# Routed rows of a mixture-of-experts layer: scattered into slot order, or gathered by block from token order

## The chip, the cores and the metric

One core of a Trainium2 chip, one launch. The metric is the device time of that core in microseconds (us). The kernel runs cross-attention and a mixture-of-experts feed-forward layer on 2048 tokens of width 512, four batches of 512.

## The reference, cut to what matters

```python
x = x + xattn(_layernorm(x), ctx_1024, ...)        # 16 heads, not touched by the change
xt = _layernorm(x).reshape(-1, 512)                # N = 2048 tokens
gate = xt @ Wr + br                                # 7 routed experts
_, ids = jax.lax.top_k(gate + gate_bias, 2)        # two experts for each token
probs = softmax(gate at ids, -inf elsewhere)
for e in range(7):                                 # e-th routed expert
    u = xt @ Wup[e] + bup[e]
    g = silu(u @ Wgate[e] + bgate[e]) * u
    eo[e] = g @ Wdown[e] + bdown[e]
out = sum_e probs[:, e] * eo[e] + shared_expert(xt)   # one shared expert of the same form
x = x + out
```

The kernel computes an expert only for the tokens that chose it: 4096 rows, grouped by expert and padded to blocks of 128, at most 38 blocks.

## The kernel before, in words

Five stages follow one another with a barrier of all engines after each: `project` (projections of the attention), `attend` (scores, softmax, values), `output` (output projection, second layer norm, routing, and the shared expert for the first eight tiles of tokens), `routed` (38 blocks of routed expert work) and `late` (the shared expert for the other eight tiles, and the sum of everything). There is no planner: each engine has its own instruction list, written out by hand, and semaphores join them.

In `output`, TensorE multiplies tile by tile (16 tiles of 128 tokens; `attended`, `turn`, `scores`). VectorE (DVE) writes the normed rows of a tile into `xn2` (L1311). Then TensorE does the shared expert in two groups of four tiles: `up` (8 products), `prefix` (two small products that count tokens by expert), `gate(0, c)`, `gate(1, c)` and `down(0, j)`, `down(1, j)`, c and j from 0 to 3, each of 12 matmuls of 128x512 (L1515). A `down(0, j)` waits for all four `gated_low(0, c)` of DVE (L1357). DVE has, in this order: the logits and the two maxima, a long chain of small operations that ends in `slot` (L1429, the place of each token's two rows in the array sorted by expert), `up_low(1, 3)`, `gated` and `gated_low` of group 0, the tables of blocks (L1438 to L1445), the same of group 1, and `down`. ScalarE (ACT) alternates `gate` and `gated_hi`. GpSimd (POOL) waits for `slot` and issues 32 indirect DMAs (L1241), each of which scatters a tile's 128 rows of `xn2` into `xs_dram`, and waits until they have landed. `xs_dram` has 38 x 128 rows; the rows of padding slots have to be zero, so in `attend` SyncE (SP) writes 38 blocks of zeros to it (L816) from a zero tile.

In `routed`, SP loads block n of `xs_dram` (256 KB, L1628) into one of two buffers. TensorE's step n (L1773) is: `up` product of block n (12 matmuls), half of `down` of block n - 2, transposes of block n - 1's `g` and of block n's `u`, the other half of `down`, then the four transposes of the rows of block n + 1 (`psX`, L1753; they wait for the load), and the `gate` product of block n. ACT's L1690 copies each transposed block out of PSUM. POOL meanwhile loads the experts' weights and splits each into two half-precision parts: 42 halves of a matrix (experts 2 to 7 and the shared one again, seven times six), for each the pieces L193, L197, L198, L201 and then the load of the half after next (L183) in the same queue. Four experts' worth (24 halves) are in a hardware loop with one operation more (L1674); the last 18 are written out. A block's first product waits for the split of its expert. The last copy of the shared expert waits for 16 blocks (L1684). SP stores a block's result to `ys_dram`; `late` gathers from there with 32 indirect DMAs (L1887) of the same kind as the new ones.

Of the kernel before, what the change touches and what calls it, by code (L numbers as in the profile page):

```python
# [21 lines left out]
F32 = mybir.dt.float32  # L22
F16 = mybir.dt.float16
# [35 lines left out]
UNROLL = 4  # L59
E_EARLY = 2  # L60
# [26 lines left out]
def build(nc, t, out, upto=99, dbg=None):  # L87
# [17 lines left out]
    with ctx:  # L105
# [5 lines left out]
        xs_dram = dram("xs_dram", (NSLOT, D), F32)  # L111
# [13 lines left out]
        CONST = 2848 + 256 + 2 * HD * 4 + 2 * 32  # L125
# [11 lines left out]
        blk_w = const("blk_w", [P, NBLK], I32)  # L137
        ws_tile = const("ws_tile", [P, 1], F32)
# [7 lines left out]
        wo = nc.alloc_sbuf_tensor_at("wo", [P, 2, KD, D], F16, offset=WO_AT)  # L146
        V_AT = (WO_AT - V_BYTES) // 32 * 32
# [3 lines left out]
        zero = nc.alloc_sbuf_tensor_at("zero", [P, D], F32, offset=O_AT + (B - 1) * KD * 2 * S * 2)  # L151
# [22 lines left out]
        xs_zeroed = sem("xs_zeroed")  # L174
# [570 lines left out]
def attend(nc, t, sem, g_):  # L745

    ident_b, ones, v_all, oT_all, q_stk, k_stk, q_hi, k_hi, zero, loaded, hi_loaded = (
        g_[k] for k in "ident_b ones v_all oT_all q_stk k_stk q_hi k_hi zero stk_loaded hi_loaded".split())
# [21 lines left out]
    zeroed = sem("a_zeroed")  # L770
    CLEAR_AT = 2 * G

    with ExitStack() as ps:  # L773
# [18 lines left out]
        @block.sync  # L792
        def _(sp):
            pair = TB // PAIR - 1
            for buf, dst, done, parts in ((g_["q_st"], q_dram, g_["qk_stored"][0], (0, 0, 1)), (g_["k_st"], k_dram, g_["qk_stored"][1], (0, 1, 0))):
                for r, part in enumerate(parts):
                    d = dst[r, (B - 1) * D:B * D, pair * PAIR * P:(pair + 1) * PAIR * P]
                    sp.dma_start(d.rearrange("(c p) t -> p c t", p=P), buf[:, pair, part]).then_inc(done[pair], 16)
            for u in range(N):
                if u == 2 * G - 1:  # L800
                    for q in g_["qk_stored"][0] + g_["qk_stored"][1]:
                        sp.wait_ge(q, 3 * 16 * NT // PAIR // 2)
                n = u - CLEAR_AT
                if n == 0:
                    sp.wait_ge(zeroed, 1)
# [12 lines left out]
            sp.wait_ge(g_["split_done"], len(early) + 1)  # L818
            sp.dma_start(raw[:, 0, :], t["x"].rearrange("b s d -> (b s) d")[0:P, :]).then_inc(g_["x0_loaded"], 16)
            sp.dma_start(raw[:, 1, :], t["L0_xattn_bo"].partition_broadcast(P)).then_inc(g_["bo_loaded"], 16)  # L820

        @block.gpsimd
        def _(pool):

            pool.memset(nm[:, :, :, :], 0.0).then_inc(s["nm0"], 1)
            pool.memset(zero[:, :], 0.0).then_inc(zeroed, 1)
            pool.wait_ge(zeroed, 1)
# [46 lines left out]
        def _(act):  # L874
# [17 lines left out]
            def hi_part(gr):  # L892
                b, c = divmod(gr, KD)
                act.wait_ge(s["o_sum"], gr + 1)
                if b == B - 1 and c == 0:
                    act.wait_ge(g_["xs_zeroed"], 16 * NBLK)
# [183 lines left out]
def output(nc, t, sem, g_):  # L1080

    w_exp, ident, oT_all, wo, slot, prob, pmat, blk_k, blk_w, b_up, b_gate = (
        g_[k] for k in "w_exp ident oT_all wo slot prob pmat blk_k blk_w b_up b_gate".split())
# [55 lines left out]
    sqrt_first = sb("sqrt_first", [P, 1], F32)  # L1139
    names = """r_loaded bo_copied br_loaded col_loaded xb_r y_mm x1_r stats aggr veps sd_r rs_r xn_r nT_t nT_c r_mm logit  # L1140
        xT_h xT_l u_mm u_r u_h u_l g_mm silu g_r g_h g_l d_mm d_r
        const0 const1 iota member prefix exp_in exp slots probs scattered"""
# [15 lines left out]
    with ExitStack() as ps:  # L1158
# [16 lines left out]
        def _(sp):  # L1175
# [42 lines left out]
        def _(pool):  # L1218
# [6 lines left out]
            pool.iota(bidx_i[:, :], pattern=[[1, NBLK]], base=0, channel_multiplier=0).then_inc(s["iota"], 1)  # L1225
            pool.wait_ge(s["const0"], 1)
# [71 lines left out]
        def _(dve):  # L1298
# [35 lines left out]
            for n in range(NT + 2):  # L1334
                if n == TB:
                    dve.wait_ge(s["iota"], 2)
                    link(dve.tensor_copy(ramp[:, :], ramp_i[:, :]))
                    link(dve.tensor_copy(bidx[:, :], bidx_i[:, :]))
                    dve.wait_ge(s["bo_copied"], 1)
# [131 lines left out]
        def _(pe):  # L1471
# [102 lines left out]
def routed(nc, t, sem, g_):  # L1574

    w_exp, blk_k, blk_w, ident, seen, ws_tile, bias = (
        g_[k] for k in "w_exp blk_k blk_w ident seen ws_tile bias".split())
    tag = "e_"
    N = NBLK
    sb = Map(nc, SBUF_LO + E * g_["PER_E"], g_["AUX_AT"])  # L1580
    x_in = sb(tag + "x", [P, 2, D], F32)
# [9 lines left out]
    x_ld = [sem(tag + "x_loaded0"), sem(tag + "x_loaded1")]  # L1591
# [23 lines left out]
    with ExitStack() as ps:  # L1615
# [6 lines left out]
        def _(sp):  # L1622
# [36 lines left out]
        def _(pool):  # L1659
# [436 lines left out]
```

## Time and profile before

| | us |
|---|---|
| three runs | 1059.81, 1060.17 (median), 1060.41 |
| the profiled execution: its time | 1063.63 |
| its span, from first to last instruction | 1062.0 |
| mean granted TensorE clock | 0.96 of full |

A row of instructions gives the line, the engine, the operation and the tiles it writes and reads, and then counts and times. A name with a q (POOLq, SPq) is the engine's own sequencer: barriers, branches, the issue of DMAs. A DMA's time to landing is from its issue until its semaphore has risen. All times in rows are us from the start of the span, unless marked ns.

### The profile page before, as it was taken

How to read it: one execution, taken by the hardware profiler on the slowest of the kernel's cores; microseconds unless marked ns; L12 is line 12 of the kernel's file. 1: busy time of each engine (PE TensorE's matmuls, PEld its weight loads, DVE VectorE, ACT ScalarE, POOL GpSimd, SP SyncE). 2: the span in 40 equal slices, each digit the busy share in tenths (PEclk: the TensorE clock that was granted, in tenths of full speed). 3: DMA queues.
4: the chain of work that ended last, by engine and by line, in shares of the span. 5: the costliest groups of instructions: out<-in, count | busy, mean ns of one | idle time of the engine just before them, and what ended most of it. 6: DMA issues, size and time to landing. Idle time of an engine off the chain costs nothing. (4 is left out here: it accounts for less than half of the span.)

```text
span 1062.0 us, 17127 instructions
## 1 busy us (share of the span) xinstructions
PE 925.9 (87%) x5077; PEld 404.0 (38%) x5078; DVE 653.6 (62%) x1022; ACT 464.8 (44%) x844; POOL 614.1 (58%) x554
## 2 busy tenths in 40 slices
PE   1789894698988988879999389999999999999898
PEld 1345452111111211136644134454455444554343
DVE  5877774777877878447766145455545545443288
ACT  2365663667767777622353012322232223232440
POOL 0465556257667676443107488899899999000660
PEclk9899997599999999989999689999999999999899
DMA  7134445234444431123325754565556655444763
GB/s 262 35 103 132 137 135 168 70 134 175 146 170 166 142 110 62 51 72 134 132 83 219 278 159 159 186 198 176 177 180 198 187 175 171 119 119 179 279 198 139
DMA packets 104521, 162.31 MB, mean 153 GB/s; under 512 B 10904, under 2 KB 53912, under 8 KB 104080
## 3 DMA queue, kind: packets, MB, share of 16 engines
q1 hardware_dynamic: 90240, 115.13, 34.1%
q0 software_dynamic: 12896, 45.10, 12.2%
q10 hardware_dynamic: 1328, 1.36, 0.4%
q8 instruction: 30, 0.49, 0.2%
q14 instruction: 27, 0.22, 0.1%
HBM read 108.08 MB, written 53.48 MB: 152 GB/s over the span
## 5 line engine op out<-in xcount | busy, mean ns | idle before, releaser
L933 DVE TENSOR_REDUCE nm<-a_psS 128x4 bf16<-128x1984 f32 x64 | 142.7, 2229 | 63.8 <-PE a_psS L992 61.9
L890 ACT ACTIVATE p_t<-a_psT 128x512 f32<-128x512 f32 x256 | 138.9, 595 | 64.8 <-PE a_psT L1009 63.1
L843 POOL TENSOR_TENSOR p_sum<-p_t,p_t 128x512 f32<-128x512 f32 x64 | 81.4, 1273 | 93.6 <-ACT p_t L890 92.7
L1763 PE MATMUL e_psU<-w_exp,e_xT 128*128 x456 | 107.4, 386 | 7.6 <-issue 3.4
L1763 PE MATMUL e_psY<-w_exp,e_gT 128*128 x456 | 110.7, 379 | 0.9 <-ACT e_y L1704 0.9
L1763 PE MATMUL e_psG<-w_exp,e_uT 128*128 x456 | 106.5, 384 | 2.5 <-DVE e_uT L1718 2.5
L201 POOL TENSOR_TENSOR w_exp<-e_raw,w_exp 128x1024 f32 (+1 forms) x42 | 90.1, 2144 | 6.0 <-POOL e_raw L198 4.5
L1009 PE MATMUL a_psT<-q_stk,k_stk 98*128 98x512 f16 x256 | 85.8, 400 | 4.0 <-ACT p_t L890 1.5
L193 POOL TENSOR_TENSOR w_exp<-e_raw,ws_tile 128x1024 f32 (+1 forms) x42 | 80.2, 1909 | 6.1 <-DMA e_raw<-in_L_ffn_Wup_dram 5.2
L1690 ACT ACTIVATE e_gT<-e_psGT 128x512 f16<-128x512 f32 x38 | 22.7, 597 | 125.1 <-PE e_psGT L1753 125.1
L1745 DVE TENSOR_TENSOR e_g<-e_g,e_u 128x512 f32<-128x512 f32 x38 | 58.8, 1547 | 26.4 <-ACT e_g L1711 26.4
L1711 ACT ACTIVATE e_g<-e_g 128x512 f32<-128x512 f32 x38 | 23.9, 630 | 107.8 <-DVE e_g L1721 107.8
L1763 PEld LDWEIGHTS e_psU<-w_exp,e_xT 128*128 128x128 f16 x456 | 42.1, 99 | 71.8 <-issue 27.9
L1016 PE MATMUL a_psO<-p_t,v_all 128*32 128x512 f32 x512 | 68.8, 611 | 0.1
L1763 PEld LDWEIGHTS e_psG<-w_exp,e_uT 128*128 128x128 f16 x456 | 42.3, 99 | 54.5 <-issue 10.4
L1763 PEld LDWEIGHTS e_psY<-w_exp,e_gT 128*128 128x128 f16 x456 | 44.5, 98 | 46.6 <-issue 1.4
L1009 PEld LDWEIGHTS a_psT<-q_stk,k_stk 98*128 98x128 f16 x256 | 17.9, 97 | 111.4 <-issue 67.3
L1241 POOL DMA_INDIRECT xs_dram<-xn,slot x32 | 31.4, 980 | 48.5 <-DVE slot L1429 39.1
L1721 DVE SCALAR_TENSOR_TENSOR e_g<-e_psG,bias 128x512 f32<-128x512 f32 x38 | 26.3, 692 | 53.7 <-PE e_psG L1763 53.7
L1718 DVE TENSOR_TENSOR e_xT<-e_psX,e_xT 128x512 f16<-128x512 f32 x38 | 26.3, 691 | 50.0 <-ACT e_xT L1690 50.0
L1718 DVE TENSOR_TENSOR e_gT<-e_psGT,e_gT 128x512 f16<-128x512 f32 x38 | 26.3, 692 | 47.8 <-ACT e_gT L1690 47.8
L1485 PE MATMUL o_psY<-wo,oT_all 128*128 128x512 f16 x192 | 45.3, 388 | 6.0 <-PEq L773 6.0
(317 smaller groups left out, 1792.8 us busy)
## 6 DMA issues: line engine op xcount, KB each, us to landing
xs_dram<-zero SPq DMA_DIRECT2D x38, 256.0 KB, 5.3
e_x<-xs_dram SPq DMA_DIRECT2D x38, 256.0 KB, 4.1
bias<-in_L_ffn_bup_dram SPq DMA_DIRECT2D x38, 256.0 KB, 3.7
bias<-in_L_ffn_bgate_dram SPq DMA_DIRECT2D x38, 256.0 KB, 3.9
ys_dram<-e_y SPq DMA_DIRECT2D x38, 256.0 KB, 4.0
q_dram<-q_st SPq DMA_DIRECT2D x24, 256.0 KB, 2.9
k_dram<-k_st SPq DMA_DIRECT2D x24, 256.0 KB, 3.7
q_stk<-q_dram SPq DMA_DIRECT2D x64, 96.0 KB
```

Source lines behind the costliest of these rows:

```text
L193: pool.tensor_tensor(hi, w, ws, ALU.mult).then_inc(w_scaled, 1)
L201: pool.tensor_tensor(lo, w, hi, ALU.subtract).then_inc(split_done, 1)
L843: pool.tensor_tensor(p_sum[:, w % SUMS, :], probs(w, 0), probs(w, 1), ALU.add).then_inc(s["sum_1"], 1)
L890: act.activation(probs(w, k), psT[:, k % 2], ACT.Exp, scale=SCALE / (QS * QS)).then_inc(s["exp"], 1)
L933: dve.tensor_reduce(nm[:, i, :, 0:1].rearrange("p h o -> p (h o)"), psS[:, :, 0:NMAIN], AX.X, ALU.max, negate=True)
L1009: pe.matmul(psT[:, k % 2], k_stk[0:KR, w % SLOTS, k * P:(k + 1) * P], q_stk[0:KR, w % SLOTS, :], start=True, stop=True).then_inc(s["t_mm"], 1)
L1016: ins = pe.matmul(dst[j * HD:(j + 1) * HD, :], stationary(n), moving(n), start=first, stop=last, tile_position=(0, j * HD))
L1241: pool.indirect_dma_start(g_["xs_dram"], bass.IndirectOffsetOnAxis(ap=slot[:, k, n:n + 1], axis=0), xn2[:, n, :], None).then_inc(s["scatte ...
L1485: ins = pe.matmul(psY[n % 2][:, :], oT_all[:, b, q, x, j * P:(j + 1) * P], wo[:, y, q, :], start=(i == 0), stop=(i == len(terms) - 1))
L1718: return dve.tensor_tensor(pair[:, 1], src[:, :].rearrange("p (k n) -> p k n", n=P), pair[:, 0], ALU.subtract)
L1745: dve.tensor_tensor(g[:, :], g[:, :], u[:, j], ALU.mult).then_inc(s["g_r"], 1)
L1763: ins = pe.matmul(dst[:, :], stationary, moving, start=(k == 0 and chunks[0] == 0), stop=(k == len(terms) - 1 and chunks[-1] == KD - 1))
```

## The change

`xs_dram`, its 38 clears, the zero tile and the 32 scatters are taken out. In their place the normed rows go to `xn_dram` in token order, tile by tile, by SP. DVE and TensorE make a table `token`: for each block (38 columns) and each row of it (128 partitions) the number of the token. It comes from one-hot matrices: with `at_row` (row of the slot, 128 columns) as stationary and `at_blk` (block of the slot times the token's number, 38 columns) as moving operand, 32 small matmuls add up the table in PSUM, after `gate(1, 2)`; DVE copies it to SBUF after `gated_low(0, 0)`. Padding slots get token 0; nothing reads their results. POOL gathers the rows of block n with an indirect DMA into `x_rows[n % 2]`: blocks 0 and 1 at the end of its `output` list, the other 36 between the halves of its weight splitting in `routed`. There POOL's loop is now written out for all 42 halves, without L1674's operation. The rows' buffers are where `wo` was.

```diff
+ROWS = 2
-        xs_dram = dram("xs_dram", (NSLOT, D), F32)
+        xn_dram = dram("xn_dram", (B * S, D), F32)
+        def gather(pool, n):
+            pool.indirect_dma_start(x_rows[:, n % ROWS, :], None, xn_dram,
+                                    bass.IndirectOffsetOnAxis(ap=token[:, n:n + 1], axis=0)).then_inc(row_ld[n % ROWS], 16)
 # attend: SP
-                if 0 <= n < NBLK:
-                    sp.dma_start(g_["xs_dram"][n * P:(n + 1) * P, :], zero[:, :]).then_inc(g_["xs_zeroed"], 16)
 # output: SP, after the store of x1 and the load of a tile
+                if n:
+                    sp.wait_ge(s["xn_r"], n)
+                    sp.dma_start(g_["xn_dram"][(n - 1) * P:n * P, :], xn2[:, n - 1, :]).then_inc(s["xn_stored"], 16)
 # output: POOL (and two iotas more at its start)
-            pool.wait_ge(g_["xs_zeroed"], 16 * NBLK)
-            pool.wait_ge(s["xn_r"], NT)
-            pool.wait_ge(s["slots"], 1)
-            for k in range(TOP):
-                for n in range(NT):
-                    pool.indirect_dma_start(g_["xs_dram"], bass.IndirectOffsetOnAxis(ap=slot[:, k, n:n + 1], axis=0),
-                                            xn2[:, n, :], None).then_inc(s["scattered"], 16)
-            pool.wait_ge(s["scattered"], 16 * TOP * NT)
+            pool.wait_ge(s["xn_stored"], 16 * NT)
+            pool.wait_ge(s["tokens"], 1)
+            for n in range(ROWS):
+                g_["gather"](pool, n)
 # output: DVE
-            dve.tensor_copy(slot[:, :, :], slot_f[:, :, :]).then_inc(s["slots"], 1)
+            link(dve.tensor_copy(slot[:, :, :], slot_f[:, :, :]))
             up_low(1, 3)
+            link(dve.tensor_scalar(in_blk_i[:, :, :], slot[:, :, :], 7, None, ALU.logical_shift_right))
+            link(dve.tensor_copy(in_blk[:, :, :], in_blk_i[:, :, :]))
+            link(dve.scalar_tensor_tensor(in_row[:, :, :], in_blk[:, :, :], -float(P), slot_f[:, :, :], ALU.mult, ALU.add))
+            for k in range(TOP):
+                dve.tensor_tensor(at_row[:, k], ... [P, NT, P], ... [P, NT, P], ALU.is_equal)
+                link(dve.tensor_tensor(at_blk[:, k], ... [P, NT, NBLK], ... [P, NT, NBLK], ALU.is_equal))
+                dve.tensor_tensor(at_blk[:, k], at_blk[:, k], tok ... [P, NT, NBLK], ALU.mult).then_inc(s["places"], 1)
             for c in range(KD):
                 gated(0, c)
                 if c:
                     gated_low(0, c - 1)
+                if c == 1:
+                    dve.wait_ge(s["places_mm"], 1)
+                    dve.tensor_copy(token[:, :], psR[:, 0:NBLK]).then_inc(s["tokens"], 1)
 # output: TensorE
+            def tokens():
+                pe.wait_ge(s["places"], TOP)
+                for k in range(TOP):
+                    for n in range(NT):
+                        ins = pe.matmul(psR[:, 0:NBLK], at_row[:, k, n, :], at_blk[:, k, n, :], ...)
+                ins.then_inc(s["places_mm"], 1)
             for c in range(KD):
                 gate(1, c)
+                if c == 2:
+                    tokens()
 # routed: SP loses load(n, j), three lines; POOL:
                         for piece in range(3):
                             g_["split_half"](...)
+                        for b in range(ROWS, N):
+                            if (b - ROWS) * 4 // 3 == (k - E_EARLY) * 2 * NM + 2 * m + half:
+                                pool.wait_ge(s["xT_t"], b - ROWS + 1)
+                                g_["gather"](pool, b)
...
-                        if not isinstance(k, int):
-                            pool.tensor_tensor(seen[:, :], ws_tile[:, :], ws_tile[:, :], ALU.add)
                         load(*((k, half, m + 1) if m < NM - 1 else (k + 1, half, 0)))
-            with pool.Fori(E_EARLY, E - 1) as k:
+            for k in range(E_EARLY, E + 1):
                 halves(k, False)
-            halves(E - 1, False)
-            halves(E, False)
             pool.wait_ge(s["y_mm"], B * S // P)
             halves(E + 1, True)
+            for b in range(ROWS, N):
+                if (b - ROWS) * 4 // 3 >= 2 * NM * (E + 2 - E_EARLY):
+                    pool.wait_ge(s["xT_t"], b - ROWS + 1)
+                    g_["gather"](pool, b)
```

## Rows read from the trace of the kernel before

**Rows 1.** The busy time of each engine by stretch; the columns stand in its first line.

```profile
core 0: us, PE busy (x) PEld busy (x) DVE busy (x) ACT busy (x) POOL busy (x), PEclk, DMA share, GB/s
592.00:607.00 15.00, 0.12 (x1) 0.12 (x2) 0.69 (x1) 0.00 (x0) 7.26 (x8) 0.58 0.56 204
607.00:985.00 378.00, 362.87 (x1824) 181.38 (x1824) 185.32 (x228) 107.42 (x190) 265.76 (x232) 0.99 0.54 171
...
607.00:612.00 5.00, 3.37 (x10) 1.48 (x11) 0.69 (x1) 0.60 (x1) 0.64 (x1) 0.50 0.90 315
```

**Rows 2.** The same view inside `attend`: beside the clears, and after them.

```profile
274.00:300.00 26.00, 22.15 (x156) 4.74 (x157) 19.26 (x23) 18.62 (x34) 18.20 (x15) 1.00 0.49 169
...
404.00:430.00 26.00, 21.87 (x157) 4.72 (x156) 19.33 (x19) 17.86 (x33) 14.59 (x12) 1.00 0.19 61
```

**Rows 3.** The end of `output` by engine (min/median/max ns, first and last start).

```profile
L1158 SPq DRAIN  x1: 7/7/7, 596.4 to 596.4; - x1
L1158 POOLq COMPARE_BRANCH  x1: 46/46/46, 601.0 to 601.0; - x1
L1158 POOLq DRAIN  x1: 2667/2667/2667, 601.2 to 601.2; - x1
```

**Rows 4.** Timeline around that end: start us, us, instructions, idle before and its releaser.

```profile
586.42 5.34 PE L1515 MATMUL o_psN<-w_exp,f_gT 128*128 128x512 f16 x24
...
592.74 0.69 DVE L1364 SCALAR_TENSOR_TENSOR o_y<-o_psN,o_x_again 128x512 f32<-128x512 f32 x1 [2.09 <-DMA x_dram<-o_y]
...
604.59 1.55 POOL L183 DMA_DIRECT2D e_raw<-in_L_ffn_Wup_dram  x2 [5.35 <-POOLq L1158]
...
606.88 1.12 PE L1753 MATMUL e_psX<-ident,e_x 128*128 128x128 f32 x4 [15.12 <-DMA e_x<-xs_dram]
...
611.36 1.88 POOL L193 TENSOR_TENSOR w_exp<-e_raw,ws_tile 128x1024 f32 x1 [5.22 <-DMA e_raw<-in_L_ffn_Wup_dram]
```

**Rows 5.** Timeline of the middle of `output`, where the table's operations go in.

```profile
558.02 1.29 DVE L1353 TENSOR_TENSOR f_g<-f_g,f_u 128x512 f32<-128x512 f32 x2
...
560.52 5.34 PE L1515 MATMUL o_psE<-f_uT,w_exp 128*128 128x512 f16 x24
...
563.43 0.39 DVE L1438 TENSOR_TENSOR cmpb<-bidx,cum_a 128x228 f32<-128x228 f32 x1
...
570.88 5.34 PE L1515 MATMUL o_psN<-w_exp,f_gT 128*128 128x512 f16 x24
```

**Rows 6.** Groups by line: busy us, mean ns of one, idle us before.

```profile
L648 DVE SCALAR_TENSOR_TENSOR wq<-wq_raw,wq 128x2048 f16<-128x2048 f32 x1 | 2.3, 2293 | 2.0 <-ACT wq L518 2.0
L999 PE MATMUL a_psX<-ident_b,nm 128*128 128x128 bf16 x64 | 6.6, 228 | 3.8 <-DVE nm L934 2.5
L1887 POOL DMA_INDIRECT l_yr<-ys_dram,slot x32 | 34.2, 1067 | 9.9 <-issue 9.9
L1241 POOL DMA_INDIRECT xs_dram<-xn,slot x32 | 31.4, 980 | 48.5 <-DVE slot L1429 39.1 <-issue 9.4
```

**Rows 7.** The landing of the 32 indirect DMAs of `late`.

```profile
DMA to landing us min/median/max: 3.4/4.1/7.9
```

**Rows 8.** L193 alone in a stretch of 15 written-out halves, first start to sixteenth.

```profile
791.92:892.89 100.97, 28.66 (x15) 1.00 0.58 183
```

**Rows 9.** Timeline of one written-out half on POOL.

```profile
811.27 0.77 POOL L183 DMA_DIRECT2D e_raw<-in_L_ffn_Wdown_dram  x1 [0.30 <-POOL w_exp L201]
812.07 1.90 POOL L193 TENSOR_TENSOR w_exp<-e_raw,ws_tile 128x1024 f16<-128x1024 f32 x1
...
815.44 2.13 POOL L201 TENSOR_TENSOR w_exp<-e_raw,w_exp 128x1024 f16<-128x1024 f32 x1
817.87 0.77 POOL L183 DMA_DIRECT2D e_raw<-in_L_ffn_Wup_dram  x1 [0.30 <-POOL w_exp L201]
```

**Rows 10.** ACT's copies of blocks 2 to 32, and TensorE's transposes of block 32.

```profile
L1690 ACT ACTIVATE e_xT<-e_psX x31: 591/591/592, 626.9 to 917.2; 128x512 f16<-128x512 f32 x31
...
916.51 0.60 PE L1753 MATMUL e_psX<-ident,e_x 128*128 128x128 f32 x4
```

More of the change, by code:

```diff
@@ L124, in build @@
         O_BYTES = B * KD * 2 * S * 2
-        CONST = 2848 + 256 + 2 * HD * 4 + 2 * 32
+        CONST = 2848 + 256 + 2 * HD * 4 + 2 * 32 + 160
         const = Map(nc, SBUF_HI - CONST, SBUF_HI)
@@ L137, in build @@
         blk_w = const("blk_w", [P, NBLK], I32)
+        token = const("token", [P, NBLK], I32)
         ws_tile = const("ws_tile", [P, 1], F32)
@@ L146, in build @@
         wo = nc.alloc_sbuf_tensor_at("wo", [P, 2, KD, D], F16, offset=WO_AT)
+        x_rows = nc.alloc_sbuf_tensor_at("x_rows", [P, ROWS, D], F32, offset=WO_AT)
         V_AT = (WO_AT - V_BYTES) // 32 * 32
@@ L150, in build @@
         oT_all = nc.alloc_sbuf_tensor_at("oT_all", [P, B, KD, 2, S], F16, offset=O_AT)
-        zero = nc.alloc_sbuf_tensor_at("zero", [P, D], F32, offset=O_AT + (B - 1) * KD * 2 * S * 2)
         half_sb = Map(nc, SBUF_LO, V_AT)
@@ L173, in build @@
         hi_loaded = [sem(f"hi_loaded{n}") for n in range(2)]
-        xs_zeroed = sem("xs_zeroed")
+        row_ld = [sem(f"rows_loaded{n}") for n in range(ROWS)]
         split_done = sem("w_split_done")
@@ L745, in attend @@
 def attend(nc, t, sem, g_):
-    ident_b, ones, v_all, oT_all, q_stk, k_stk, q_hi, k_hi, zero, loaded, hi_loaded = (
-        g_[k] for k in "ident_b ones v_all oT_all q_stk k_stk q_hi k_hi zero stk_loaded hi_loaded".split())
+    ident_b, ones, v_all, oT_all, q_stk, k_stk, q_hi, k_hi, loaded, hi_loaded = (
+        g_[k] for k in "ident_b ones v_all oT_all q_stk k_stk q_hi k_hi stk_loaded hi_loaded".split())
     q_dram, k_dram = g_["q_dram"], g_["k_dram"]
@@ L769, in attend @@
     raw_ld = sem("a_raw_loaded")
-    zeroed = sem("a_zeroed")
-    CLEAR_AT = 2 * G
     with ExitStack() as ps:
@@ L825, in _ @@
             pool.memset(nm[:, :, :, :], 0.0).then_inc(s["nm0"], 1)
-            pool.memset(zero[:, :], 0.0).then_inc(zeroed, 1)
-            pool.wait_ge(zeroed, 1)
+            pool.wait_ge(s["nm0"], 1)
             pool.memset(k_stk[K3:KR, :, :], QS).then_inc(s["sel"], 1)
@@ L894, in hi_part @@
                 act.wait_ge(s["o_sum"], gr + 1)
-                if b == B - 1 and c == 0:
-                    act.wait_ge(g_["xs_zeroed"], 16 * NBLK)
                 if b == B - 1 and c == 1:
@@ L1080, in output @@
 def output(nc, t, sem, g_):
-    w_exp, ident, oT_all, wo, slot, prob, pmat, blk_k, blk_w, b_up, b_gate = (
-        g_[k] for k in "w_exp ident oT_all wo slot prob pmat blk_k blk_w b_up b_gate".split())
+    w_exp, ident, oT_all, wo, slot, prob, pmat, blk_k, blk_w, b_up, b_gate, token = (
+        g_[k] for k in "w_exp ident oT_all wo slot prob pmat blk_k blk_w b_up b_gate token".split())
     low = Map(nc, SBUF_LO + E_EARLY * g_["PER_E"], g_["O_AT"])
@@ L1139, in output @@
     sqrt_first = sb("sqrt_first", [P, 1], F32)
+    row_i = sb("row_i", [P, P], I32)
+    row = sb("row_f", [P, P], F32)
+    tok_i = sb("tok_i", [P, NT], I32)
+    tok = sb("tok_f", [P, NT], F32)
+    in_blk_i = sb("in_blk_i", [P, TOP, NT], I32)
+    in_blk = sb("in_blk", [P, TOP, NT], F32)
+    in_row = sb("in_row", [P, TOP, NT], F32)
+    at_row = sb("at_row", [P, TOP, NT, P], F16)
+    at_blk = sb("at_blk", [P, TOP, NT, NBLK], F16)
     names = """r_loaded bo_copied br_loaded col_loaded xb_r y_mm x1_r stats aggr veps sd_r rs_r xn_r nT_t nT_c r_mm logit
         xT_h xT_l u_mm u_r u_h u_l g_mm silu g_r g_h g_l d_mm d_r
-        const0 const1 iota member prefix exp_in exp slots probs scattered"""
+        const0 const1 iota member prefix exp_in exp slots probs xn_stored places places_mm tokens"""
     s = {n: sem("o_" + n) for n in names.split()}
@@ L1225, in _ @@
             pool.iota(bidx_i[:, :], pattern=[[1, NBLK]], base=0, channel_multiplier=0).then_inc(s["iota"], 1)
+            pool.iota(row_i[:, :], pattern=[[1, P]], base=0, channel_multiplier=0).then_inc(s["iota"], 1)
+            pool.iota(tok_i[:, :], pattern=[[P, NT]], base=0, channel_multiplier=1).then_inc(s["iota"], 1)
             pool.wait_ge(s["const0"], 1)
@@ L1335, in _ @@
                 if n == TB:
-                    dve.wait_ge(s["iota"], 2)
+                    dve.wait_ge(s["iota"], 4)
                     link(dve.tensor_copy(ramp[:, :], ramp_i[:, :]))
                     link(dve.tensor_copy(bidx[:, :], bidx_i[:, :]))
+                    link(dve.tensor_copy(row[:, :], row_i[:, :]))
+                    link(dve.tensor_copy(tok[:, :], tok_i[:, :]))
                     dve.wait_ge(s["bo_copied"], 1)
@@ L1428, in _ @@
                 link(dve.tensor_reduce(slot_f[:, k, :], prod[:, :, :], AX.X, ALU.add))
-            dve.tensor_copy(slot[:, :, :], slot_f[:, :, :]).then_inc(s["slots"], 1)
+            link(dve.tensor_copy(slot[:, :, :], slot_f[:, :, :]))
             up_low(1, 3)
+            link(dve.tensor_scalar(in_blk_i[:, :, :], slot[:, :, :], 7, None, ALU.logical_shift_right))
+            link(dve.tensor_copy(in_blk[:, :, :], in_blk_i[:, :, :]))
+            link(dve.scalar_tensor_tensor(in_row[:, :, :], in_blk[:, :, :], -float(P), slot_f[:, :, :], ALU.mult, ALU.add))
+            for k in range(TOP):
+                dve.tensor_tensor(at_row[:, k], row[:, :].unsqueeze(1).broadcast_to([P, NT, P]),
+                                  in_row[:, k, :].unsqueeze(2).broadcast_to([P, NT, P]), ALU.is_equal)
+                link(dve.tensor_tensor(at_blk[:, k], bidx[:, :].unsqueeze(1).broadcast_to([P, NT, NBLK]),
+                                       in_blk[:, k, :].unsqueeze(2).broadcast_to([P, NT, NBLK]), ALU.is_equal))
+                dve.tensor_tensor(at_blk[:, k], at_blk[:, k], tok[:, :].unsqueeze(2).broadcast_to([P, NT, NBLK]), ALU.mult).then_inc(s["places"], 1)
             for c in range(KD):
@@ L1560, in _ @@
             up(0, 3)
+            def tokens():
+                pe.wait_ge(s["places"], TOP)
+                for k in range(TOP):
+                    for n in range(NT):
+                        ins = pe.matmul(psR[:, 0:NBLK], at_row[:, k, n, :], at_blk[:, k, n, :],
+                                        start=(k == 0 and n == 0), stop=(k == TOP - 1 and n == NT - 1))
+                ins.then_inc(s["places_mm"], 1)
             for c in range(KD):
@@ L1574, in routed @@
 def routed(nc, t, sem, g_):
-    w_exp, blk_k, blk_w, ident, seen, ws_tile, bias = (
-        g_[k] for k in "w_exp blk_k blk_w ident seen ws_tile bias".split())
+    w_exp, blk_k, blk_w, ident, seen, ws_tile, bias, x_in, x_ld = (
+        g_[k] for k in "w_exp blk_k blk_w ident seen ws_tile bias x_rows row_ld".split())
     tag = "e_"
     N = NBLK
-    sb = Map(nc, SBUF_LO + E * g_["PER_E"], g_["AUX_AT"])
-    x_in = sb(tag + "x", [P, 2, D], F32)
+    sb = Map(nc, SBUF_LO + E * g_["PER_E"], g_["WO_AT"])
     xT = sb(tag + "xT", [P, 2, 2, KD, P], F16)
@@ L1590, in routed @@
     s = {n: sem(tag + n) for n in names.split()}
-    x_ld = [sem(tag + "x_loaded0"), sem(tag + "x_loaded1")]
     raw_ld = [sem("e_raw_loaded0"), sem("e_raw_loaded1")]
@@ L1624, in rows @@
                 return g_[name][ds(n * P, P), :]
-            def load(n, j):
-                at_least(sp, s["xT_t"], n - 1)
-                sp.dma_start(x_in[:, j], rows("xs_dram", n)).then_inc(x_ld[j], 16)
             def biases(n):
@@ L1637, in step @@
             def step(n, j, i):
-                if not isinstance(n, int) or n + 2 < N:
-                    load(n + 2, j)
                 if live(n, -1):
@@ L1649, in step @@
                     sp.dma_start(g_["of_first"][:, :, :], g_["x1_dram"][0:NBASE * P, :].rearrange("(n p) d -> p n d", p=P)).then_inc(late_ld, 16)
-            load(0, 0)
             biases(0)
-            load(1, 1)
             run(sp, step)
```

3 lines of the change are left out of this document (removed).

## The prediction, made before the changed kernel was run

> **What bounds the kernel now.** I read the busy times by stretch first. In `routed`, 378 of the 1062 us of span, TensorE is busy 362.87 us at a granted clock of 0.99: its own work bounds the stage. POOL is busy 265.76 us there and has slack only because it stops early (of its 42 halves the last but one begins at 892.89) [rows 1, 8]. The one large hole is ahead of it: from 592 to 607 TensorE does 0.12 us of work [rows 1]. The view of the stage's end shows who is late: TensorE ends at 591.8, DVE at 593.4, SP reaches the barrier at 596.4, but POOL sees its scatters landed only at 601.0 and then drains for 2.67 us [rows 3, 4]. Then SP issues the load of block 0 and TensorE starts at 606.88 [rows 4]. So the scatters cost TensorE about 8 us past SP's end, plus nearly 3 us for a load that could have been made before. After the hole the granted clock is 0.50, the lower of its two levels, 1.2 of 2.4 GHz, from 607 to 612 [rows 1].
>
> **The clears.** 38 writes and SP's issues vanish from `attend`. Beside them TensorE is busy 22.15 of 26 us, after them 21.87, at one clock [rows 2]: they were hidden by TensorE's and DVE's work, and nothing comes back. I take 0; both signs of 1 us are possible.
>
> **The rows' stores and the constants.** 16 DMA issues of SP and two iotas fall beside tile work that TensorE bounds; SP waits there for DVE, not the reverse. Taken as 0, at most 1 us.
>
> **The table on DVE.** Ahead of `gated(0, 0)` come two operations of 128x2048 at 2.29 us [rows 6], four of 128x608 and three small ones. The 608 columns lie between 228 at 0.39 and 512 at 0.69 [rows 5] and above: 0.8 each. With 0.2 for each small one that is 4.6 + 3.2 + 0.6 = 8.4 us. Less than 4 would need half the price of each row, more than 10 a disturbed DVE. So `gated(0, 0)` moves from 558.0 to 566.4 [rows 5].
>
> **The table on TensorE.** 32 matmuls with a weight load each. The nearest row is L999's, 0.228 us for one of 128 columns; such matmuls overlap, and four transposes take 0.60 together with the end of the last [rows 6, 10], so some 0.11 each. I take 0.107, 3.4 us in all; the ends are 3.2 and 32 x 0.228 = 7.3. TensorE comes to them after `gate(1, 2)` at 560.5 + 7.8 = 568.3, when DVE is done at 566.4, ends at 571.7, and `gate(1, 3)` at 574.3. DVE stands at its wait with `gated(0, 2)`, `gated(0, 3)` and all of group 1 behind it. It goes on at 571.9 and needs two pairs of 1.4 us and the last `gated_low`: 575.4. `down(0, 0)` waits for that, so it starts at 575.4 instead of 570.88 [rows 5]: 4.5 us later. Group 1's `gated` (6.5 us from 578.3) is ready just before `down(1, 0)` at 585.8. TensorE ends at 591.8 + 4.5 = 596.3.
>
> **The boundary.** The last `down` of DVE ends near 597.0. DVE had waited 2.1 us for stores that shared the DMAs with the scatters [rows 4]; that cover is gone, and a store should land in some 2.3 us. SP ends at 599.3. POOL has nothing outstanding, so no long drain. Its load came 0.7 us after its drain's end before [rows 3, 4]: 600.1 now, against 604.59, 4.5 us earlier. TensorE has its rows already and starts at 599.9, 7.0 us earlier. With a shorter hole the lower clock should cost about 1.5 us less (it now takes some 5). By TensorE alone the sum would be -8.5 us.
>
> **The gathers, and what is late next.** POOL had 42 halves; now 36 gathers stand between them or behind. The loop's extra operation goes, so all halves cost what the written-out ones do: 100.97 / 15 = 6.73 us [rows 8]. Of one gather, `late` shows 1.067 us busy and 9.9 / 32 = 0.31 idle before it, pitch 1.36 beside a busy DVE; the scatters show 0.98 + 0.30 [rows 6, 7]. Behind L201 the load waits 0.30 for its completion [rows 9], and a gather in between could cover that. So a gather adds 0.98 at least and 1.45 at most; I take 1.3, near the pitch, as I see nothing that makes the sequencer's pause overlap.
>
> The gather of block b stands behind half (b - 2) x 4 // 3: the gaps are one, one and two halves. Three blocks therefore cost POOL 4 x 6.73 + 3 x 1.3 = 30.8 us. TensorE needs (917.2 - 626.9) / 30 = 9.68 us a block, 29.0 for three [rows 10]. POOL is the slower by 1.8 us every three blocks, and TensorE comes to wait, at its `psX` transposes, for blocks 5, 8, 11 and so on; all it does afterwards is behind that wait, the `gate` product first. Block 32's gather (b - 2 = 30) stands behind half 40, the last one that comes after a pair. POOL's first split follows its load by 6.77 us [rows 4], at 606.9. The gather of block 2 follows that split by 5.8, at 612.7. That of block 32 follows by 40 x 6.73 + 30 x 1.3 = 308.2: 920.9. It lands 3.8 us later (3.4 to 4.1 in rows 7): 924.7. Before, these transposes began at 916.51 [rows 10]. So TensorE is 8.2 us later there, not 8.5 earlier. Block 33's gather is one half later and no wait; the last four follow without a half between them. The remainder and `late` keep their length. The weights' splits slow down too: six halves and four or five gathers are 46 us an expert, against 2 x 2048 / 7 = 585 rows, five padded blocks and 48 us of TensorE. The second expert is split at 606.9 + 46 = 653, and the first one's five or six blocks end near 650 to 658: at most a wait of a few us, which the rows' later waits would swallow. The rows bind.
>
> The Trainium skill, in "DMA: Bandwidth & Descriptors", section "Anatomy of one DMA — SWDGE (gpsimd) path", speaks against this: it calls descriptor generation "small, variable" and says that many descriptors can be emitted before it shows. By that rule a gather would cost POOL next to nothing and the sum would be rival 1's. Of this the trace says otherwise: POOL is held for about a microsecond by each indirect DMA [rows 6], so I stay with the rows.
>
> Sum, against the profiled execution: span 1062.0 + 8.2 = 1070.2, and with its 1.6 us around the span 1071.8 in place of 1063.63. The median of the runs is 3.5 us below the profiled time; the same step from 1060.17 gives 1068.4 us.
>
> **Rivals.** (1) POOL keeps up and the gain stays. For it: slack in POOL of 80 us at the end, and a loop's overhead removed. It needs 4h + 3g below 29.0 us and an early lead, as with g = 0.98 and h = 6.55. Then TensorE bounds as before: -8.5, 1051.7. With g = 0.98 and h = 6.73 the price falls by 30 x 0.32 = 9.6: -1.4, a result of no size. (2) POOL is dearer still: a gather at 1.45 and the weight load behind it in the same queue landing late, since a half's load has 7.4 us [rows 9] and the gather's 256 KB go first. The price is 30 x 0.15 = 4.5 and 40 x 0.1 = 4: 1077. It decides from the first block on which TensorE waits, near block 5. [...] (3) The table doesn't shorten the boundary: the stage's end stays near 604, since SP's last store or a drain after the two gathers takes the place of the scatters. Against it: the gathers are issued near 572. It would add 3 to 4 us to the forecast, within its range.
>
> **How the numbers follow.** The forecast's own range, +3 to +12 (1063 to 1072), has 0.53; rival 1 with its lesser gains, -9 to -2, 0.27; rival 2 0.14; 0.06 is left for sums near zero. A change of under 0.2% (2 us) can't be told from none. Faster: 0.28, same 0.05, slower 0.67. The range takes in most of rivals 1 and 2: 1052 to 1077.
>
> **What would show it.** Right: the hole ahead of `routed` some 4 us of TensorE instead of 15; TensorE waiting about 2 us for `x_rows` at every third block and at no other; POOL busy without idle time to some 930; the last `down` of `output` near 596. Wrong: TensorE's pitch at 9.7 with no waits on `x_rows`, or halves with a gather not over 1.1 us longer than those without. If TensorE waits at the `up` product for L201 instead, the splits bind and not the rows.

## The result

| | before | changed |
|---|---|---|
| median of the runs, us | 1059.66 (1057.32 to 1061.35, 20 runs) | 1061.61 (1060.85 to 1064.79, 20 runs) |
| the profiled execution: time, span | 1063.63, 1062.0 | 1063.08, 1061.3 |

The ratio is 1.0023, 95% interval 1.0015 to 1.0031: 2 us slower. The forecast was 8.2 us slower, 1068.4. The direction held by a hair, and a later repeat can't tell it from no change (1.0007, below). The size did not hold: 6.8 us too high. The measured time lies inside the stated range of 1052 to 1077, which is wide enough for most outcomes.

First the busy times of the changed kernel by stretch, in the columns of [rows 1]:

```profile
592.00:607.00 15.00, 7.97 (x29) 3.30 (x28) 3.46 (x5) 0.60 (x1) 2.67 (x3) 0.77 0.63 190
607.00:985.00 378.00, 355.58 (x1813) 178.89 (x1811) 182.53 (x227) 107.10 (x188) 298.84 (x244) 1.00 0.52 167
607.00:612.00 5.00, 3.16 (x18) 1.66 (x17) 1.98 (x3) 1.09 (x2) 4.59 (x5) 1.00 0.39 144
```

The hole has shrunk: TensorE has 7.97 us of work in those 15, where it had 0.12. It then has 7.3 us less work in `routed` in the same 378 us, and POOL 33 us more. The granted clock from 607 to 612 is full, not half.

Next, the middle of `output` in the changed kernel, as a timeline (it answers to [rows 5]). L1444 to L1448 are the table on DVE, L1586 is the table on TensorE, L1456 its copy, and the last row is `down(0, 0)`.

```profile
560.64 2.29 DVE L1444 TENSOR_TENSOR at_row<-row_f,in_row 128x2048 f16<-128x2048 f32 x1
...
562.85 0.78 DVE L1446 TENSOR_TENSOR at_blk<-bidx,in_blk 128x608 f16<-128x608 f32 x1
...
568.11 1.28 DVE L1362 TENSOR_TENSOR f_g<-f_g,f_u 128x512 f32<-128x512 f32 x2
...
570.13 0.97 PE L1586 MATMUL o_psR<-at_blk,at_row 128*128 128x38 f16 x32
...
571.14 0.20 DVE L1456 CAST token<-o_psR 128x38 int32<-128x38 f32 x1 [0.96 <-PE o_psR L1586]
...
574.67 1.67 PE L1536 MATMUL o_psN<-w_exp,f_gT 128*128 128x512 f16 x7 [0.98 <-DVE f_gT L1366]
```

Then the barrier of `output` by engine (it answers to [rows 3]), and the timeline around it (to [rows 4]):

```profile
L1164 POOLq DRAIN  x1: 5051/5051/5051, 572.4 to 572.4; - x1
...
L1164 SPq DRAIN  x1: 7/7/7, 600.7 to 600.7; - x1
```

```profile
597.70 0.69 DVE L1373 SCALAR_TENSOR_TENSOR o_y<-o_psN,o_x_again 128x512 f32<-128x512 f32 x1 [1.40 <-DMA x_dram<-o_y]
...
600.95 1.09 PE L1776 MATMUL e_psX<-ident,x_rows 128*128 128x128 f32 x4 [5.40 <-PEq L1164]
601.37 1.51 POOL L185 DMA_DIRECT2D e_raw<-in_L_ffn_Wup_dram  x2 [26.60 <-POOLq L1164]
...
605.85 1.89 POOL L195 TENSOR_TENSOR w_exp<-e_raw,ws_tile 128x1024 f16<-128x1024 f32 x1 [2.96 <-DMA e_raw<-in_L_ffn_Wup_dram]
...
611.50 1.06 POOL L217 DMA_INDIRECT x_rows<-xn_dram,token  x1 [0.17 <-issue]
```

SP, not POOL, now ends the stage; POOL's drain of 5 us lies at 572, hidden. TensorE starts at 600.95 instead of 606.88.

Inside `routed`, POOL's timeline (it answers to [rows 9]): a half with a gather, and below the dots the start of one without. After it the window of L195 alone, 16 halves with 12 gathers (to [rows 8]).

```profile
790.56 2.13 POOL L203 TENSOR_TENSOR w_exp<-e_raw,w_exp 128x1024 f16<-128x1024 f32 x1
792.85 1.32 POOL L217 DMA_INDIRECT x_rows<-xn_dram,token  x1 [0.17 <-issue]
794.17 0.76 POOL L185 DMA_DIRECT2D e_raw<-in_L_ffn_Wgate_dram  x1
794.96 1.91 POOL L195 TENSOR_TENSOR w_exp<-e_raw,ws_tile 128x1024 f16<-128x1024 f32 x1
...
816.49 0.77 POOL L185 DMA_DIRECT2D e_raw<-in_L_ffn_Wdown_dram  x1 [0.30 <-POOL w_exp L203]
```

```profile
787.18:907.64 120.46, 30.49 (x16) 1.00 0.54 174
```

And who waits: TensorE's waits in `routed` (us in total, times, longest), and after it, from the timeline, the gather of block 32 and its transposes (to [rows 10]).

```profile
PE e_psX L1776 <- DMA x_rows<-xn_dram,token: 7.2, 7, 1.8
PEld e_psX L1776 <- DMA x_rows<-xn_dram,token: 11.9, 10, 2.3
PE e_psGT L1776 <- DVE e_g L1768: 5.1, 7, 1.1
```

```profile
913.32 1.32 POOL L217 DMA_INDIRECT x_rows<-xn_dram,token  x1 [0.17 <-issue]
...
917.34 0.66 PE L1776 MATMUL e_psX<-ident,x_rows 128*128 128x128 f32 x4 [0.69 <-DMA x_rows<-xn_dram,token]
```

PEld is TensorE's weight load, which comes just ahead of the matmul. It waits for the rows at ten blocks: 5, 8, 11 and so on to 32, every third and no other. From its first split (605.85) to the gather of block 32 POOL itself never waits longer than 0.3 us. Block 32's transposes start at 917.34, where they started at 916.51: TensorE began `routed` 5.9 us earlier and is 0.8 us later here. So POOL's list of halves and gathers is the bound, and a gain of some 6 to 8 us was given back in it.

In these two profiled executions what follows is 1.5 us shorter than before, so the spans differ by -0.7; the medians differ by +2.0. The size has to come from the medians: a second trace of the kernel before (the repeat below) has block 32's transposes at 913.54 and a span of 1056.0, where the first has 916.51 and 1062.0. A second trace of the changed kernel starts `output` 2.9 us later (469.3 against 466.3), and its span is 1064.0.

### The profile page after: what moved, and what is told of

Read it like the earlier page. It is cut to its first block and busy times, and to the rows that moved or that the text cites. A ratio compares the mean times of both kernels' runs of the same rounds, so it can differ in the third digit from the quotient of the medians.

```text
span 1061.3 us, 16869 instructions
## 1 busy us (share of the span) xinstructions
PE 924.7 (87%) x5109; PEld 404.3 (38%) x5110; DVE 659.5 (62%) x1034; ACT 464.9 (44%) x844; POOL 617.9 (58%) x537
## 3 DMA queue, kind: packets, MB, share of 16 engines
q10 hardware_dynamic: 1328, 1.36, 0.4%
## 5 line engine op out<-in xcount | busy, mean ns | idle before, releaser
L203 POOL TENSOR_TENSOR w_exp<-e_raw,w_exp 128x1024 f16<-128x1024 f32 x42 | 90.0, 2143 | 3.5
L217 POOL DMA_INDIRECT x_rows<-xn_dram,token x38 | 43.0, 1131 | 78.8 <-DVE token L1456 50.5
L195 POOL TENSOR_TENSOR w_exp<-e_raw,ws_tile 128x1024 f16<-128x1024 f32 x42 | 80.0, 1906 | 4.0 <-DMA e_raw<-in_L_ffn_Wup_dram 3.0
L1768 DVE TENSOR_TENSOR e_g<-e_g,e_u 128x512 f32<-128x512 f32 x38 | 56.5, 1488 | 26.4 <-ACT e_g L1734 26.4
```

The source lines that it names most:

```text
L195: pool.tensor_tensor(hi, w, ws, ALU.mult).then_inc(w_scaled, 1)
L203: pool.tensor_tensor(lo, w, hi, ALU.subtract).then_inc(split_done, 1)
L1768: dve.tensor_tensor(g[:, :], g[:, :], u[:, j], ALU.mult).then_inc(s["g_r"], 1)
```

## The experiments

Theory A, after the result: POOL binds in `routed` as forecast, but a gather costs it less than the 1.3 us taken. Theory B: POOL doesn't bind, and the loss comes from elsewhere (shared DMAs, the written-out loop, the removed clears).

**One gather per 1.25 halves, or per 1.5.** Only the places of the gathers move; POOL has the same work in total.

```diff
-                            if (b - ROWS) * 4 // 3 == (k - E_EARLY) * 2 * NM + 2 * m + half:
+                            if (b - ROWS) * 5 // 4 == (k - E_EARLY) * 2 * NM + 2 * m + half:
```

(The same in the condition of the last gathers. The other kernel has `3 // 2` at both places.)

> The changed kernel with each gather one place earlier on average: block b's gather stands behind half (b - 2) x 5 // 4 instead of x 4 // 3; the work is the same. Theory (GpSimd's pace holds TensorE in the routed stage): four blocks then cost GpSimd 5 x 6.73 + 4 x 1.07 = 37.9 us against TensorE's 38.7, so TensorE never waits for rows; block 32's transposes come about 9.5 us earlier than in the kernel before and the time is 8 to 10 us below the changed kernel, near 1052. Rival (the gain is lost to slower gathers or other contention of the DMAs, not to the order on GpSimd): within 2 us of the changed kernel, as the same transfers are made. Rival (the weights' splits bind once they are later): waits of the up product for L203, a gain of under 5 us.

> The changed kernel with the gathers rarer: behind half (b - 2) x 3 // 2. Theory: two blocks cost GpSimd 3 x 6.73 + 2 x 1.07 = 22.3 us against 19.4 of TensorE, so TensorE waits some 2.9 us at every second block from block 4 or 6 on, and is 28 us later at block 32 than in the kernel before: 27 to 29 us over the changed kernel, near 1089. Rival (the DMAs, not the order): no change within 2 us.

Measured: with 5 // 4 1051.82 us, ratio 0.9936 (0.9923 to 0.995); with 3 // 2 1089.5 us, ratio 1.0283 (1.0269 to 1.0298). The waits of TensorE in `routed` of the kernel with 3 // 2:

```profile
PE e_psX L1776 <- DMA x_rows<-xn_dram,token: 26.9, 13, 3.4
```

With 5 // 4 this list has no row for `x_rows`. One constant moves the time by 10 us down or 28 up from the changed kernel, both as expected, so where the gathers stand in POOL's list decides: theory A. Not all of the 10 us are waits for rows: from the changed kernel to 5 // 4 these fall from 7.2 us to none, and TensorE's waits for DVE's product (`e_psGT`) from 5.1 to 0.9. Why the product is faster there is taken up in the last section.

**The rows loaded by SP instead of gathered.** In place of all gathers SP loads 128 consecutive rows of `xn_dram` (the wrong tokens, so the routed part is computed from other rows); the table is still made.

```diff
-                                g_["gather"](pool, b)
+                        sp.dma_start(x_in[:, j], g_["xn_dram"][ds((n + 2) * 48, P), :]).then_inc(x_ld[j], 16)
```

> The changed kernel with no gather at all: SyncE loads each block's 128 rows in one piece from the stored rows, at the place where the kernel before loaded them (the rows are not those of the block's tokens, so the outputs differ). The table is still made. Theory: GpSimd has only its halves (6.73 us each), TensorE bounds the routed stage, and the time is that of e1, 1050 to 1053. Rival (the loss is in the output stage or at its end): within 2 us of the changed kernel.

Measured: 1052.68 us, ratio 0.994 (0.9926 to 0.9954). Its POOL timeline, load and first piece of two neighbouring halves:

```profile
787.50 0.78 POOL L185 DMA_DIRECT2D e_raw<-in_L_ffn_Wdown_dram  x1 [0.30 <-POOL w_exp L203]
788.31 1.91 POOL L195 TENSOR_TENSOR w_exp<-e_raw,ws_tile 128x1024 f16<-128x1024 f32 x1
...
794.12 0.78 POOL L185 DMA_DIRECT2D e_raw<-in_L_ffn_Wdown_dram  x1 [0.30 <-POOL w_exp L203]
794.92 1.91 POOL L195 TENSOR_TENSOR w_exp<-e_raw,ws_tile 128x1024 f16<-128x1024 f32 x1
```

Here a half takes 6.74 us in the mean over the written-out loop (6.61 in these rows); in the changed kernel 120.46 / 16 = 7.53 with three gathers to four halves. So a gather costs POOL (7.53 - 6.74) / 0.75 = 1.06 us. Behind a gather the load has no wait of 0.30, and the gather's own pause is 0.17. And with the gathers gone TensorE keeps its gain: this kernel and the one with 5 // 4 lie within 1 us of each other (within 2 us of its repeat below).

**Before, with POOL's loop written out.** The hardware loop goes, and its extra operation with it, and nothing else.

```diff
-            with pool.Fori(E_EARLY, E - 1) as k:
+            for k in range(E_EARLY, E + 1):
```

> The kernel before with GpSimd's loop over four experts written out, as the change has it, and nothing else. Theory: GpSimd isn't what TensorE waits for there, so the halves get shorter (7.2 to 6.7 us) and the time stays within 1.5 us of the kernel before. Rival (the written-out loop itself costs, through its code): over 2 us slower.

Measured: 1061.16 us, ratio 1.0014 (1.0005 to 1.0023). The halves that were in the loop fell from 7.23 to 6.73 us, as forecast for the changed kernel, but before that wasn't the bound: a faster POOL alone brings nothing. The time rose by 1.8 us, 0.3 more than expected, and I can't place that. The changed kernel has the same written-out loop, so part of its own +2.0 may come from there; no run separates the two.

**Four kernels on another chip.** The next four ran on a chip on which the kernel before takes 1100.91 us (1098.36 to 1103.94, 11 runs), so they are compared with each other: from the changed kernel with the clears put back (last of the four) to the others.

Plain loads on POOL in place of the 36 gathers of `routed` (consecutive rows, so again the wrong tokens):

```diff
-                                g_["gather"](pool, b)
+                                pool.dma_start(x_in[:, b % ROWS], g_["xn_dram"][b * 48:b * 48 + P, :]).then_inc(x_ld[b % ROWS], 16)
```

> The changed kernel with the 36 gathers of the routed stage replaced by plain loads of 128 stored rows in one piece, issued by GpSimd at the same places (the rows are not those of the block's tokens, so the outputs differ). Theory: only the gather's price on GpSimd differs, some 0.78 us instead of 1.07; three blocks cost it 4 x 6.73 + 3 x 0.78 = 29.3 us against TensorE's 29.0, so TensorE hardly waits and the time is 7 to 9 us below the changed kernel, 1053 to 1055. Rival (the wait is for the landing of the rows, any transfer on this queue behind the splits): under 2 us below the changed kernel.

One small operation on POOL behind each gather:

```diff
                                 g_["gather"](pool, b)
+                                pool.tensor_tensor(seen[:, :], ws_tile[:, :], ws_tile[:, :], ALU.add)
```

> The changed kernel with one small GpSimd operation more behind each gather of the routed stage (128x1, like L199: 0.19 us and a gap of some 0.08), which brings a gather's share from the measured 1.07 to 1.34 us, near the 1.3 that was forecast. Theory (the forecast's only wrong term was this price): block 32 comes 30 x 0.27 = 8 us later and the time is 7 to 9 us over the changed kernel, 1069 to 1071. Rival (TensorE's waits absorb it, or other terms were wrong by as much): under 4 us over.

The table later, behind `gated` of group 0 on DVE and in `down(0, 1)` on TensorE, with 5 // 4:

```diff
-                if c == 2:
-                    tokens()
...
+                if j == 1:
+                    tokens()
```

> Experiment e1 (gathers behind half (b - 2) x 5 // 4) with the table made later: DVE's operations for it come after group 0's gated_low, its matmuls after down(0, 1), and DVE copies the table after group 1's gated_low. Theory: down(0, 0) no longer waits for the table (about 2 us from e1, 1.0 of it matmuls that stay), so the output stage ends 1 to 2 us earlier and the time is 1 to 2 us below e1, near 1050.5. Rival (group 1's gated_low becomes what down(1, 0) waits for): the same as e1 or up to 2 us slower.

The clears and their zero tile put back into `attend`:

```diff
+                if 0 <= n < NBLK:
+                    sp.dma_start(g_["xs_dram"][n * P:(n + 1) * P, :], zero[:, :]).then_inc(g_["xs_zeroed"], 16)
```

> The changed kernel with the 38 clears of an unused array put back into the attention stage, with their zero tile, issues and the wait of ScalarE for them. Theory: they are hidden, so the time is that of the changed kernel within 1 us. Rival (the removal of 10 MB of writes had given something back, or had moved the stage's end, which is 1.3 us later in the changed kernel's trace): over 1.5 us from the changed kernel.

Measured: 1079.01, 1092.98, 1080.75 and 1087.68 us; ratios to before 0.9793 (0.9769 to 0.9817), 0.9928 (0.9912 to 0.9945), 0.9806 (0.9777 to 0.9835), 0.9885 (0.9863 to 0.9906). Plain loads are 8.7 us below the kernel with the clears, as expected. The small operation is 5.3 above it, not 7 to 9, but not under 4 either. POOL's timeline of these two kernels, the plain load first, shows why:

```profile
787.61 0.61 POOL L1693 DMA_DIRECT2D x_rows<-xn_dram  x1
788.22 0.71 POOL L185 DMA_DIRECT2D e_raw<-in_L_ffn_Wgate_dram  x1
788.95 1.91 POOL L195 TENSOR_TENSOR w_exp<-e_raw,ws_tile 128x1024 f16<-128x1024 f32 x1
```

```profile
792.78 1.07 POOL L217 DMA_INDIRECT x_rows<-xn_dram,token  x1 [0.17 <-issue]
793.86 0.21 POOL L1694 TENSOR_TENSOR seen<-ws_tile 128x1 f32<-128x1 f32 x1
793.99 0.76 POOL L185 DMA_DIRECT2D e_raw<-in_L_ffn_Wgate_dram  x1
```

The added operation is 0.21 us long, but the load behind it starts 0.13 after it, not 0.21 or more: it overlaps too. Over 30 gathers 0.13 makes 3.9 us. Counted from the first split, block 32's copy comes 4.4 us later than in the kernel with the clears, and 3.2 later than in the changed kernel on the first chip. This is POOL's bound tested by a dose: what is added per gather comes back some 30 times at block 32. The whole time is the weaker measure here, since on this chip the two traces also differ by 4 us after block 32.

The clears: in the stretch of `attend` beside them (274 to 300, columns as in [rows 1]), first the kernel that has them back, then the changed one:

```profile
274.00:300.00 26.00, 22.12 (x160) 4.72 (x156) 19.33 (x21) 18.57 (x35) 18.99 (x16) 1.00 0.49 169
```

```profile
274.00:300.00 26.00, 22.17 (x160) 4.74 (x160) 19.26 (x23) 18.60 (x35) 17.76 (x15) 1.00 0.32 107
```

The DMA share falls from 0.49 to 0.32, TensorE's work stays. At the end of `output` SP is at the barrier at 600.7 in both. The clears were hidden. (The two traces are of two chips; up to the end of `routed` their times agree within 1.3 us.)

Where the other chip loses: busy times of the kernel with the clears there from 1008 to 1036, and of the changed kernel on the first chip.

```profile
1008.00:1036.00 28.00, 13.50 (x29) 2.93 (x29) 5.31 (x8) 6.14 (x10) 16.30 (x17) 0.58 0.59 169
```

```profile
1008.00:1036.00 28.00, 27.68 (x129) 12.38 (x128) 22.85 (x34) 12.76 (x21) 18.39 (x18) 1.00 0.68 203
```

It lies in `late`: 29 matmuls where the first chip does 129, one to three at a time with gaps of up to 2.2 us of "issue" before them. In the plain-load kernel it is the same stretch (46 matmuls at a clock of 0.61). Why, and why the kernel before loses some 41 us on that chip and the changed one less, stays open: the kernel before has no trace from there.

**Before again, the changed kernel again, 5 // 4 again, and the table later, on the first chip.** The kernels are those above, without a further edit.

> The kernel before, unchanged, for its trace on the chip of this comparison: e5 to e8 ran where the kernel before took 1100.91 us, e1 to e4 where it took 1059.36. Theory: TensorE's instructions come late where the DMAs are saturated, on the slower chip far more than on the faster; there the trace shows gaps between TensorE's matmuls of over 1 us in the late stage (some 22 us, as in e8) and also in the output stage while the scatters run (12 to 18 us, which the changed kernel doesn't have). On a chip with 1059 neither shows. Rival (the slower chip is slower everywhere): every stage is longer by 2 to 4%.

> The changed kernel, unchanged. Theory: where the kernel before takes near 1059 us, it takes 1.5 to 3 us more; where that takes near 1101, the changed kernel takes 10 to 14 us less (near 1088), since the scatters' share of the late instructions is gone. Rival: the same ratio of 1.002 on both.

> e1 again, beside e12 and e10 on one chip. Theory: 8 to 10 us below e10 on either chip, as TensorE's wait for rows is the same on both. Rival: only on the faster.

> e7 again, the table made later and the gathers at 5 // 4, beside e11 on the same chip. Theory: 1 to 2 us below e11, since down(0, 0) doesn't wait for the table. Rival (down(1, 0) waits instead, or SyncE's last stores bound the stage's end): within 1 us of e11 or above.

Measured: before 1059.86 (ratio to itself 1.0005, 0.9991 to 1.0019); changed 1061.69 us, ratio 1.0007 (0.9992 to 1.0022), here not to be told from no change; 5 // 4 1050.95 us, ratio 0.9932 (0.9908 to 0.9957), the best version, 10.7 below the changed kernel where 8 to 10 were expected; table later 1057.23 us (12 runs, 1051.14 to 1063.73), ratio 0.9984 (0.9963 to 1.0005). The last was expected just below 5 // 4 and is 6 us above. `down(0, 0)` did come earlier, 13.5 us after `slot` instead of 15.5, but this gain was lost, and more with it, in two places. First at the end of `output`, DVE's timeline:

```profile
583.28 1.29 DVE L1373 SCALAR_TENSOR_TENSOR o_y<-o_psN,o_x_again 128x512 f32<-128x512 f32 x2
588.06 0.69 DVE L1373 SCALAR_TENSOR_TENSOR o_y<-o_psE,o_x_again 128x512 f32<-128x512 f32 x1 [3.49 <-DMA x_dram<-o_y]
```

The same wait is 1.61 us in the trace of 5 // 4 taken beside it. The first two gathers now issue at 581.8 and 583.2, beside these stores, not at 570.5 and 572.1. Block 4 is 3.1 us later than in that trace (1.0 of it is there at `slot` already), but only 0.8 later than in the first trace of 5 // 4, where one of these waits was 2.7 us without a gather beside it. So this first loss is not clear of the spread, and that the gathers cause it is not shown. Second in `routed`, the same kernel's timeline of POOL, DVE and TensorE:

```profile
815.82 1.07 POOL L217 DMA_INDIRECT x_rows<-xn_dram,token  x1 [0.16 <-issue]
...
816.44 3.69 DVE L1769 TENSOR_TENSOR e_g<-e_g,e_u 128x512 f32<-128x512 f32 x1 [0.69 <-ACT e_g L1735]
...
816.89 0.75 POOL L185 DMA_DIRECT2D e_raw<-in_L_ffn_Wdown_dram  x1
817.67 1.91 POOL L195 TENSOR_TENSOR w_exp<-e_raw,ws_tile 128x1024 f16<-128x1024 f32 x1
...
820.19 0.66 PE L1777 MATMUL e_psGT<-ident,e_g 128*128 128x128 f32 x4 [1.00 <-DVE e_g L1769]
```

DVE's product of two SBUF tiles takes 0.69 us alone; this one ends 0.55 us after POOL's L195. Four blocks have one of 3.5 to 3.7, each makes TensorE some 1.2 us late, and from block 4 to block 32 this kernel takes 4.6 us more than the 5 // 4 one (272.8 against 268.2), whose products are 2.7 at most and make TensorE wait nowhere between these blocks. The first trace of 5 // 4 takes 268.2 as well, so this second loss does stand out. The traces show it; no run undoes it.

## Why the prediction was wrong, point by point

**Right.** The clears cost nothing. The table on DVE: 8.4 us forecast, 559.99 to 568.11 = 8.1 measured. The boundary: SP at 600.7 (599.3 forecast), TensorE at 600.95 (599.9), POOL's load at 601.37 (600.1): 1.0 to 1.4 us late each. `slot` was already 1.8 us later than in the trace before. 1.3 of it is there at the first product of `output`, which starts between 464.8 and 469.3 in the traces taken, with and without the clears. The drain that was not to be long took 5 us, but at 572, where it hides. The cover by the scatters was not all that held DVE: its stores still make it wait 1.4 to 1.6 us.

The lower clock (0.50) was over at 606.9, 6.0 us after TensorE's start; before it lasted until 614.8, 7.9 us, and came back for some 3.4 us after 618. By my estimate, half of such a stretch is lost: 3.0 us against 5.6, so 2.6 less instead of the 1.5 forecast. By TensorE alone the sum was -8.5, and the two kernels in which POOL doesn't bind measure -7.5 (5 // 4, first time), -8.6 (again) and -6.7 (rows by SP).

The mechanism of the loss was right as well: POOL is busy throughout, and TensorE waits at `psX` for gathers at exactly the blocks named, 5, 8, 11 to 32 (ten waits of its weight loads, up to 2.3 us).

**Off, without weight.** The table on TensorE took 0.97 us where I took 3.4: `down(0, 0)` is 2.0 us later, counted from `slot`, and not 4.5. The stores at the end of `output` and the later `slot` ate the difference, so that the boundary came out within 1.4 us is partly luck. POOL's first split came 4.5 us behind its load instead of 6.8; the rows of block 0, which loaded beside it before, no longer do, though no run shows that this is why. So the first gather is at 611.50, not 612.7, 1.2 us of the miss.

**The step that failed** is a term of the sum: "So a gather adds 0.98 at least and 1.45 at most; I take 1.3, near the pitch, as I see nothing that makes the sequencer's pause overlap." A gather adds 1.06 to 1.07 (1.03 to 1.10 by the same sum in the other traces with gathers). It is busy for 1.13 in the mean (40.7 us for 36), but the pause before it is 0.17 between computing operations, not 0.31 as between gathers [rows 6], and the load behind it no longer waits 0.30 for L203 [rows 9]. That makes 1.00; the last 0.06 isn't placed. Both overlaps were weighed in the prediction: the load's wait gave its lower end, and the pause's was rejected for want of a row. From POOL's first gather to block 32's the forecast had 40 x 6.73 + 30 x 1.3 = 308.2 us; measured 913.32 - 611.50 = 301.8, which is 40 halves of 6.74 and 30 gathers of 1.07. With the 1.2 of the start and 4.0 for the landing (3.8 taken) block 32's transposes are at 917.34, not 924.7: all of the 7.4 us. With 1.07 put in, the same sum gives +1.3 for the profiled execution in place of +8.2; the medians say +2.0.

At this price three blocks cost POOL 30.1 us against 29.0 of TensorE, so small errors count 30-fold; the prediction's own sign of being wrong ("halves with a gather not over 1.1 us longer") came true (7.71 us in the mean against 6.98 for the others in the same trace) while its sign of being right (the waits) did too. The case lay between the forecast and rival 1's "result of no size", and it got 0.06.

The Trainium skill ("DMA: Bandwidth & Descriptors", section "Anatomy of one DMA — SWDGE (gpsimd) path") calls the making of descriptors "small, variable". The runs show that a gather takes 1.07 us of GpSimd's list, enough to decide the kernel; how much of that is the making of descriptors, no run shows.

**Rivals.** Rival 1 is what happens with 5 // 4 or without gathers, not in this kernel. (Its example, g = 0.98 and h = 6.55, makes 29.14 and so misses its own condition of 29.0 by a little.) Rival 2 is excluded: a gather cost 1.07 in the mean, not 1.45, and from the first gather to block 32's no split waited for its load. Rival 3: the stores of SP did take the scatters' place at 600.7, 1.4 us above the forecast and not 3 to 4.

## What to carry to other kernels

Price an operation that goes into a busy engine's list by what it adds to the period, not by its pitch among its own kind: pauses before it and waits behind it can fall together (here 1.07 us, where the pitch was 1.36). Where two engines' periods are this close (30.1 and 29.0 us), the places of the inserted operations are worth more than the change itself: one constant, 4 // 3 to 5 // 4, gave 10 us. Put them densely enough that each is done before its consumer comes: here one per 1.25 halves was, one per 1.33 was not.

## What the runs showed of the hardware

- DVE's product of two SBUF tiles (128x512, float32) took 0.69 us, or up to 3.8 when POOL was at work. In the traces of the changed kernel and of 5 // 4 each longer one (0.8 us and more) ends 0.53 to 0.56 us after a computing operation of POOL, mostly the one that ran when it started. The mean is 1.49 in the changed kernel and 1.21 to 1.25 with 5 // 4, where the starts fall otherwise. It changes between two runs of one kernel as well: 1.55 and 1.04 in the two traces of the kernel before. POOL pays as well: L203 took 2.45 instead of 2.13 and a gather 1.33 instead of 1.07 when a product that overlapped it had started first. The Trainium skill ("SBUF — State Buffer", section "SBUF: two separate sides") has the two engines share a port pair as an exclusive lock, also for a DVE operation with two SBUF inputs; the trace agrees with that. The longest four in the kernel with the later table start in the last 0.3 to 0.45 us of a gather and end only after the load and the L195 behind it; the changed kernel has four such too. Why they are held already there, no run shows.
- 32 matmuls with 38 moving columns and a weight load each took 0.97 us together.
- Two chips differ by 41 us on the kernel before and by about 26 on the changed one (there measured with the clears in it), nearly all of it after 988 us in the traces that there are. A ratio from one chip isn't that of another: 1.0023 here, 0.9885 (with the clears) there.
